# Token and language tower kernel: turning token tiles with TensorE's transposing form on the whole array, from a second copy of the normed tokens

## What is computed

```python
h = tok(x, itok...)          # Fourier features -> 128 hidden, relu -> 64, layernorm, + 0.1 * residual
h = h + attn(layernorm(h))   # q: 8 heads x 64; k, v: one head of 64; softmax(q k^T / sqrt(8)) v; Wo
h = h + ffn(layernorm(h))    # router (relu 32, softmax, top 2), six experts 64-64-64-64, weighted sum
...
k = jnp.einsum('bsc,oc->bos', x, Wk)
v = v_conv.reshape(b, s, KD)            # the flat [64, 512] block read again as [512, 64]
out = jnp.einsum('bcp,oc->bop', ctx, Wo)
```

## Time and profile before

| | |
|---|---|
| median of 3 runs | 660.96 us (659.64 to 661.63) |
| the profiled execution, its own time | 661.2 us |
| its span in the profile | 659.3 us |
| PE busy | 632.8 us (96%) |
| DVE / ACT / POOL busy | 529.0 / 476.6 / 278.7 us |
| TensorE clock granted, mean | 0.998 of 2.4 GHz |
| one body in the steady part | 77.4 us |

### The profile page before, as it was taken

The page is one execution under the profiler, slowest core; times in us unless marked ns, Lnnn a source line. Parts: engine busy times, 40 slices in busy tenths (PEclk is TensorE's granted clock), DMA queues, the critical chain, the costliest instruction groups (busy, mean ns, idle before and its releaser), DMA issues.

```text
span 659.3 us, 27475 instructions
## 1 busy us (share of the span) xinstructions
PE 632.8 (96%) x11948; PEld 363.8 (55%) x11948; DVE 529.0 (80%) x1069; ACT 476.6 (72%) x1215; POOL 278.7 (42%) x357
## 2 busy tenths in 40 slices
PE   7799999999999999999999999999999999999985
PEld 6355555546655565455665466555565556555663
DVE  6787877888697977979788887979869797878666
ACT  3888874986679775896658866787668966688543
POOL 2341313516463093623835155530836229131184
PEclk9999999999999999999999999999999999999999
DMA  5000000000000001000100001000010000000001
GB/s 179 2 2 2 2 3 3 3 2 3 18 2 3 2 2 19 2 2 3 19 2 2 2 3 20 2 2 2 3 19 1 3 3 6 15 2 2 3 4 34
DMA packets 9720, 6.79 MB, mean 10 GB/s; under 512 B 8704, under 2 KB 9088, under 8 KB 9472
## 3 DMA queue, kind: packets, MB, share of 16 engines
q1 hardware_dynamic: 9312, 4.77, 3.0%
q10 hardware_dynamic: 288, 0.27, 0.1%
HBM read 2.93 MB, written 2.10 MB: 8 GB/s over the span
## 4 chain that ended last, share of the span: by engine, by line
PE 84%; ACT 6%; DVE 6%; issue 2%; DMA 1%; POOL 0%; SPq 0%; ACTq 0%; DVEq 0%; POOLq 0%
PE s_bank L613 33%; PE s_bank L579 29%; ACT p L915 4%; PE s_bank L712 3%; PE s_bank L804 3%; PE s_bank L793 3%; PE s_bank L830 3%; DVE nmax L1090 3%; PE s_bank L593 3%; PE s_bank L724 1%; PE s_bank L690 1%; PE s_bank L624 1%; DMA e2t<-ids 1%; PE s_bank L642 1%; ACT g L921 1%
## 5 line engine op out<-in xcount | busy, mean ns | idle before, releaser
L915 ACT ACTIVATE p<-s_bank,nmax 128x512 f32<-128x512 f32 x512 | 347.5, 693 | 134.5 <-DVE nmax L1090 129.4
L1090 DVE TENSOR_REDUCE nmax<-s_bank 128x1 f32<-128x512 f32 x512 | 323.2, 681 | 42.0 <-PE s_bank L579 41.3
L579 PE MATMUL s_bank<-kf,g 64*64 64x512 f32 x2048 | 256.5, 591 | 1.6 <-ACT p L915 1.4
L613 PE MATMUL s_bank<-p,woz 64*64 64x256 f32 x4096 | 246.0, 377 | 2.9 <-ACT p L915 2.9
L613 PEld LDWEIGHTS s_bank<-p,woz 64*64 64x64 f32 x4096 | 158.2, 133 | 108.2 <-issue 31.1
L416 POOL TENSOR_TENSOR woz<-cst,rz 128x256 f32<-128x256 f32 x126 | 74.7, 614 | 243.0 <-DVE rz L1096 243.0
L579 PEld LDWEIGHTS s_bank<-kf,g 64*64 64x64 f32 x2048 | 75.6, 133 | 88.0 <-issue 38.3
L915 ACT ACTIVATION_READ_ACCUMULATOR p<-s_bank,nmax 128x1 f32 x512 | 107.0, 209 | 0.0
L1102 DVE STREAM_TRANSPOSE m<-s_bank 128x512 f32<-128x512 f32 x64 | 45.8, 716 | 36.4 <-PE s_bank L613 36.4
L1451 POOL TENSOR_TENSOR st<-st,power 128x8 f32<-128x8 f32 (+3 forms) x25 | 38.6, 1544 | 37.4 <-DVE st L1117 37.4
L425 POOL TENSOR_TENSOR y<-y,gt 128x768 f32<-128x768 f32 x28 | 41.3, 1474 | 2.8 <-DVE y L1361 2.8
(11 more groups left out here) (133 smaller groups left out, 522.5 us busy)
## 6 DMA issues: line engine op xcount, KB each, us to landing
tower_out<-o SPq DMA_DIRECT2D x16, 128.0 KB, 2.8
cst<-consts SPq DMA_DIRECT2D x1, 1102.0 KB, 8.6
e2t<-ids SPq DMA_DIRECT2D x1, 768.0 KB, 6.0
cst<-consts SPq DMA_DIRECT2D x1, 352.0 KB, 6.4
cst<-consts ACTq DMA_DIRECT2D x1, 256.0 KB, 3.7
e2t<-ids SPq DMA_DIRECT2D x1, 192.0 KB, 3.6
cst<-consts SPq DMA_DIRECT2D x1, 128.0 KB, 3.4
e2t<-ids SPq DMA_DIRECT2D x1, 64.0 KB, 2.1
```

The costliest lines, as they stand in the source:

```text
L579: last = pe.matmul(double[half(q), 512 * r:512 * r + 512], g[half(r), a // 2 % 2, a % 2, first:first + 64], kf[half(r), par, a // 4, :], s ...
L613: last = pe.matmul(bank("PV", i, a)[half(q), 512 * hh:512 * hh + 256], woz[half(r), kept, 2 * mm + hh, :], keys[:, q, :, :], start=(part = ...
L915: nc.scalar.activation(p[:, 8 * kept + c % 8, :], bank("S", i, c - r)[:, 512 * r:512 * r + 512], ACT.Exp, bias=nmax[:, c % 16:c % 16 + 1], ...
L1090: nc.vector.tensor_reduce(nmax[:, c % 16:c % 16 + 1], bank("S", i, c - r)[:, 512 * r:512 * r + 512], AX.X, ALU.max, negate=True).then_inc( ...
```

## The change

`turned` from pair 2 on, and the turn of `x2`, use PE's transposing form on the whole 128x128 array, 8 instructions in place of 32 and 4 in place of 16. A block of 128 tokens x 128 columns is turned at once. So that both halves of the partitions get the channels, the columns must hold the 64 channels twice: `xn` becomes `[128, 8, 2, 64]`, POOL writes copy 0, and a DMA on SP's queue (`twin`), inside SBUF, copies it to copy 1, 256 KB in 1024 pieces of 256 bytes. For `x2` two neighbouring tiles are turned together, which needs no second copy. The turn of `xn`, its copies out and the step V move four slots later (T 39 to 43, V 41 to 45; in body 0 T 55 to 57 and V as before). The reads of the turned banks follow the new layout.

```diff
 P = {
-    "LNB2": 35, "T": 39, "T_ACT": (39, 39), "V": 41, "V_ACT": (40, 40), "LNA2_POOL": 19, "LNB_POOL": 29,
+    "LNB2": 35, "T": 43, "T_ACT": (43, 43), "V": 45, "V_ACT": (44, 44), "LNA2_POOL": 19, "LNB_POOL": 29,
...
 P1 = {
-    "LNB2_POOL": 49, "T": 55, "T_ACT": (55, 55), "V": 63, "V_ACT": (63, 63), "TOK_ACT": 7}
+    "LNB2_POOL": 49, "T": 57, "T_ACT": (57, 57), "V": 63, "V_ACT": (63, 63), "TOK_ACT": 7}
...
-        xn = sb("xn", [128, 8, C])
+        xn = sb("xn", [128, 8, 2, C])
...
+            def twin(w):
+                sp.wait_ge(ln_sems[1][1], 3 * w)
+                sp.dma_start(xn[:, :, 1, :], xn[:, :, 0, :]).then_inc(xn_twin, 16)
+
+            twin(2)
             for u in units[:PAIRS - 1]:
+                if u.i + 3 <= PAIRS:
+                    twin(u.i + 3)
                 sp.wait_ge(y_pool, u.pool0 + 4 * W_SUM)
...
                 free("T", w)
                 double = bank("T", w)
-                for t in range(*((0, 4), (4, 8), (0, 8))[min(w, 2)]):
+                if w >= 2:
+                    pe.wait_ge(xn_twin, 16 * (w - 1))
+                    for t in range(8):
+                        last = pe.transpose(double[:, 128 * t:128 * t + 128], xn[:, t, :, :], k("ident"))
+                    last.then_inc(t_ps, 1)
+                    return
+                for t in range(4 * w, 4 * w + 4):
...
                     for t in range(t0 // 2, t1 // 2):
-                        for r in range(2):
-                            for c in range(2):
-                                last = pe.matmul(bank("XT", u.u)[half(c), 512 * r + C * t:512 * r + C * t + C],
-                                                 x2[half(r), 2 * t + c, :], k("ident")[half(r), half(r)],
-                                                 start=True, stop=True, skip_group_check=True)
+                        last = pe.transpose(bank("XT", u.u)[:, 128 * t:128 * t + 128], x2[:, 2 * t:2 * t + 2, :], k("ident"))
```

More of the change, by code:

```diff
@@ L363, in tower @@
         stored = sem("stored")
-        (rated, power_set, spare_set, sine, feats, qk_ps, qk_sb, weighed, first_dve, first_sq, first_pow, first_xn) = [
+        (rated, power_set, spare_set, sine, feats, qk_ps, qk_sb, weighed, first_dve, first_sq, first_pow, first_xn, xn_twin) = [
             sem(x) for x in ("rated", "power_set", "spare_set", "sine", "feats", "qk_ps", "qk_sb", "weighed",
-                             "first_dve", "first_sq", "first_pow", "first_xn")]
+                             "first_dve", "first_sq", "first_pow", "first_xn", "xn_twin")]
         row_set = sem("row_set")
@@ L474, in keys @@
                 return (kf[:, par, r, :].rearrange("q (d n e) -> q d n e", d=8, e=8),
-                        src.rearrange("q (n e d) -> q d n e", e=8, d=8))
-            return (kf[:, par, :, :].rearrange("q b (d t r e) -> q r b d t e", d=8, r=2, e=8)[:, r, :, :, :, :],
-                    src.rearrange("q (b t e d) -> q b d t e", b=2, e=8, d=8))
+                        bank("T", w)[:, :].rearrange("q (n r e d) -> q r d n e", r=2, e=8, d=8)[:, r, :, :, :])
+            return kf[:, par, r, :].rearrange("q (d x) -> q d x", d=8), src.rearrange("q (x d) -> q d x", d=8)
         def load(eng, n, done):
@@ L686, in turned @@
                 double = bank("T", w)
-                for t in range(*((0, 4), (4, 8), (0, 8))[min(w, 2)]):
+                if w >= 2:
[5 more added lines that the diff above has]
+                for t in range(4 * w, 4 * w + 4):
                     for r in range(2):
                         for c in range(2):
-                            last = pe.matmul(double[half(c), 512 * r + C * t:512 * r + C * t + C], xn[half(r), t, :],
+                            last = pe.matmul(double[half(c), 512 * r + C * t:512 * r + C * t + C], xn[half(r), t, 0, :],
                                              k("ident")[half(r), half(r)], start=True, stop=True,
@@ L980, in ffn @@
                     act.wait_ge(u.x2t_ps, u.n + 1)
-                    by_half = bank("XT", u.u)[:, :].rearrange("q (r x) -> q r x", r=2)[:, :, 32 * t0:32 * t1]
-                    nc.scalar.copy(xt[:, u.cols].rearrange("q (t r p) -> q r t p", r=2, p=64),
-                                   by_half.rearrange("q r (t p) -> q r t p", p=64)).then_inc(u.xt_sb, 1)
+                    nc.scalar.copy(xt[:, u.cols], bank("XT", u.u)[:, u.cols]).then_inc(u.xt_sb, 1)
                 for e in range(EP):
@@ L1187, in first_tiles @@
                 dve.wait_ge(first_pow, 2)
-                tt(xn[:, 0:4, :], centred_h, over(st[1][:, 4, 0:4]), ALU.mult).then_inc(first_xn, 1)
+                tt(xn[:, 0:4, 0, :], centred_h, over(st[1][:, 4, 0:4]), ALU.mult).then_inc(first_xn, 1)
                 reduced(dve, nc.vector, 3, 2)
@@ L1472, in prep @@
                     pool.wait_ge(t_ps, w)
-                    scale(norm_b, xn[:, tiles, :], norm_b.xc[:, tiles, :])
+                    scale(norm_b, xn[:, tiles, 0, :], norm_b.xc[:, tiles, :])
             def wide_gamma(tiles):
```

## The result

The changed kernel takes **674.04 us** (median of 4 runs, 671.51 to 675.12); the kernel before took 660.38 on the same chip. The medians are 13.7 us apart; the ratio is 1.0203, 95% interval [1.0185, 1.0222]: 12.2 to 14.7 us slower. The forecast was 670, 662 to 677.

The account below looks back on a forecast made before the run. PE was taken to bound the kernel, with 84% of the chain of waits. Steady turns of `xn` 5.8, `x2` 1.1 and body 0 1.9 made 8.8 us on the profiled 661.2, forecast 670; range 662 to 677.

Parts of the forecast that it names:

- The turn of `xn` in the steady bodies: Slots 39 to 46: products of slot 45 wait for ACT's copy of the queries; +0.97 us in six bodies, +5.8.
- the replay: Slots 39 to 46 of body 2 worked through with the new order; queries' copy ends 215.77, products start 216.05.
- Price of the transposing form: One record of 0.12 us pitch per transposition; `x2` turn 0.60 in place of 0.46, eight times, +1.1 us.
- the way back costs nothing: Changing PE from the whole array back to tiles was taken as free; only the change to it cost 0.12 us.
- The second copy: Transfer of `xn` inside SBUF takes 3.9 us of the 6.5 available before T, so hidden with 2.6 to spare.
- Body 0: Queries wait for the turn and ACT's copies of `kf`, starting 77.9 in place of 75.99: +1.9 us; instant copy +1.8.
- Sum: Whole kernel: 5.8 + 1.1 + 1.9 = 8.8 us on the profiled 661.2, giving a median of 669.8, said as 670.
- the form is dear: Rival: transposing form takes two records or 275 ns each; `x2` +5.0 us, 675 in all; chance 0.15.
- ACT keeps up: Rival: products at slot 45 wait for nothing and the turn is cheap; -3.1 us, 658; chance 0.10.
- the copy is late: Rival: the copy in SBUF takes over 6.5 us; at 8 us, 6 x 1.5 more, 679; chance 0.05.
- no more than a shift: Rival: waits partly there and caught up later, turns cost as before; within 2 us of 661; chance 0.07.

Follow-up runs that it names:

- e1: Kernel before with only the new slots (T 43, V 45; body 0 T 57), old form, no second copy: 668.49 us, ratio 1.0124.
- e6: Changed kernel with each transposition of `xn` issued twice, same output: 672.29 us, ratio 1.0164 to the kernel before.
- e3: Kernel before with the transposing form for the turns of `x2` alone: 661.33 us, ratio 1.0021.
- e4: Changed kernel with the old slots and copy 1 of `xn` written by POOL in place of the transfer: 666.56 us, ratio 1.0096 to the kernel before.
- e5: Changed kernel with the turn back in its old slots (T 39, V 41; body 0 T 55), transfer kept: 679.24 us, ratio 1.029 to the kernel before.
- e2: Kernel before with only body 0's T moved from slot 55 to 57: 662.77 us, ratio 1.0041.
- e12: Kernel before with 48 tiny two-column matmuls put ahead of the first turn: 660.81 us, ratio 1.0011.

## Why the forecast was right, and where its terms were off

- **The turn of `xn` in the steady bodies** (+0.97 each, 5.8): right, in mechanism and nearly in size. Moved by the 7.02 us by which body 2 already ran late at slot 39, the replay had the copy of the queries at 221.75, the products at 223.07, the copies of `kf` at 223.42 and V at 224.80; the trace has 221.80, 222.86, 223.46 and 224.82. What it missed: V takes 0.96 and the products 1.96 in place of 0.86 and 1.73, both behind a wait, which makes +1.06, 6.4 us in all (the products start 0.21 earlier than replayed, which takes most of it back). e1 shows that the slots alone make it, e6 that the turn lies in the wait's shadow; the forecast gave that shadow 1.8 us, and e6's turn of 1.90 stands out of it by 0.06.
- **Price of the transposing form**: one record and 0.12 us pitch forecast; one record measured, and 0.13 with the change to the whole array in it, 0.11 without (e6). The step that failed is "the way back costs nothing": it costs 0.16 (e3, e4, and the changed kernel's chain). So `x2` is +0.28 and not +0.14 each time, about 2.2 us in place of 1.1. For `xn` the way back hides behind ACT's copy.
- **The second copy** (3.9 us, hidden with 2.6 to spare): hidden, and shorter, 3.0 in the median (in body 2 it took 4.24 and landed 2.3 us ahead of the turn). The sum of pieces by their mean time was 0.9 too high. e5 shows what it costs without cover.
- **Body 0** (+1.9): +1.89 measured, and it doesn't need the transfer (e2); the forecast's +1.8 with an instant copy said so. Not forecast: another +0.58 at its end, where the chain shows the scores of body 1 behind ACT's copies of V.
- **Not in the sum at all**: the position in the instruction stream, +1.3 at the finish in body 1. Ahead of it one turn of `xn` has 8 records where it had 64; the gap after 200 records moved to after 256, and a second one came 128 records ahead of it. The loss was made by instructions that were taken away, far from the place where they stood.
- **Sum**: 8.8 forecast, 12.3 in the trace. The 3.5 between are 1.3 (finish in body 1), 0.8 (seven turns of `x2` at 1.95, where the forecast had 1.1 for all eight), 0.6 (V in body 0), 0.6 (pieces behind a wait) and 0.4 in the tail, less 0.2. The rest up to the measured 13.7 is within its interval (12.2 to 14.7). The mechanism was right; 670 fell 4 us short mainly because the sum left out three things that all cost.
- **The rivals**: "the form is dear" gave 675, the nearest number to 674, by a mechanism that isn't there: `x2` costs 0.28 and not 0.62 more. "ACT keeps up" is out by the chain, "the copy is late" by the turn's single wait of 0.9 us in seven, "no more than a shift" by e1, where the waits cost 1.06 in each body and nothing is caught up. That the number lies near a rival's says nothing for it.

## What to carry to other kernels

Replay the chains of all engines around the new slot, instruction by instruction, before moving a piece: a later slot for PE gave another engine's copy the lead, and with the form and the transfer a slot in the middle was worse than the far one. Where a wait has appeared, make the suspect twice as long: if the piece behind the wait doesn't move, it is in the shadow, and making it cheaper is worth nothing. And when a change removes many small instructions, compare the "issue" gaps in runs of very short matmuls before taking a difference of 0.3% for the change's own.

## What the runs showed of the hardware

- **Gaps without a releaser in runs of very short matmuls.** In the finish in body 1 PE goes through matmuls at about 17 ns a record (128 in 2.08 us) and then stands; over all kernels such gaps last 0.6 to 2.2 us. Counted over all of PE's matmul records from the start of the program, the gaps there come after exactly 1488, 1616 or 1744 records in all thirteen profiled kernels, always 128 records (with 128 loads) apart, whatever stands ahead; what an edit changes is which work stands at these places. In the same run, a place that falls 8, 40, 72 or 104 records behind the run's start costs nothing, and one that falls 120 or more behind it does. The queue for instructions moves a packet of 16 KB about as often (89 packets by the page for 11332 records, one for 127). In the changed kernel, from 99 to 109 us (packets, MB, share):

```profile
q8 instruction: 3, 0.05, 1.9%
```

  The reading that fits is that instructions come in pieces of fixed size, and a run that uses them up faster than they arrive comes to stand at a piece's end once what was there ahead is used up. That is inferred from places and counts; no run changed the supply itself. In all thirteen kernels PE has such gaps of over 0.4 us only in or right behind runs of small matmuls (the finish in body 1, the tail, and once the start of e12); the scores and products, which fill most of the ninety pieces, show none.
- **Change of array mode**: 0.16 us from the whole array back to 64x64 tiles, on the first piece behind (1.89 against 1.73, 1.02 against 0.86).
- **A transposition in fp32** on the whole array is one record of 278 to 286 ns in the mean, at a pitch of 0.11 us (sixteen in 1.90, eight in 1.04). With 88 of them among ordinary matmuls the granted clock read 1.00 from 20 to 640 us; the mean of 0.992 over the span comes of the first 20 (0.83) and of the end (0.95).
- **A copy inside SBUF** of 256 KB in pieces of 256 bytes took 3.0 us in the median. In four of the five kernels that have it, one of the seven took 4.2 to 4.6 (in bodies 2, 5, 3 and 2); why was not settled.
